# Third hop of a four-layer graph network: bias added on GpSimd, end rows formed in one VectorE operation, norm in place, and the output constant moved into VectorE's copy

## The chip, the cores and the metric

The kernel is one launch on one core of a Trainium2 chip. Times are microseconds (us) of that core. TensorE (PE; PEld is its weight load) multiplies and transposes and writes PSUM. VectorE (DVE), ScalarE (ACT) and GpSimd (POOL) do elementwise work; GpSimd also issues the indirect DMAs that gather and scatter rows, and SyncE (SP) issues the plain ones. "Slower" and "faster" speak of the time of the whole launch.

## The reference

Four layers work on 50,000 nodes of 128 features and 12,500 edges sorted by destination. Each is `x = x + layer(relu(layernorm(x)))`. Cut to what matters here:

```
x1 = x  + GCN3(h)          # 3 convolutions, then @ Wl + bl
m  = h[src] + edge_feats   # second layer: mean over the edges of a node,
h  = (1+eps)*h + mean(m)   # then two products with batch norms
x3 = x2 + 6 steps of  x += relu(mean(x[src]) @ Wh.T + bh)
out = x3 + (tanh(gcn_conv(h, W1, b1)) @ W2 + b2)
```

Only nodes that are the destination of an edge ("end rows") get anything but a dense product from a convolution. So the kernel treats all nodes as dense rows and computes the rows at edge ends again, by "hops" over the sorted edges.

## The kernel before, in words

Rows come in groups of 512 (four tiles of 128); "pairs" are two groups. Edges are 98 tiles of 128, in 14 iterations (`IT`) of 7 tiles, split 4 and 3 over two buffers b (`SUB`).

A first phase (to about 1200 us) runs a list of slots. Each has one dense pair (`turn`, `prod`, `rows`, `x1_rows`) and, in later slots, iterations of hops. The hops numbered 0, 1, 2 and 3 in the code are the first to fourth hop. Hop 0 has one iteration in a slot; hops 1 to 3 have two, and two slots without a hop stand ahead of each (`GAP`). The third hop (2) runs in seven slots between 820 and 1007 us, the fourth (3, "mean") in seven from 1037 us.

An iteration of a hop is: GpSimd gathers 7 tiles of neighbour rows (`h_G` and `h_M` by turns); VectorE makes messages of them (line 291) and, after TensorE's transposes, a running sum along the edges (line 315); TensorE multiplies back into `h_P` (line 326); VectorE scales by `dinvw` and adds a bias (`dve_affine`, line 335).

In the third hop the sum then gets the raw feature rows of the end node, `XD`, loaded by SyncE (`xd_load`), in a second VectorE operation (`x1_ends`, line 1279), and lands in `RS`, the resident array [128, 98, 128]. That is x1 at the edge ends. SyncE stores it; `m_moments` and `m_rstd` take its norm's statistics; ScalarE normalizes it into a buffer `HR` (`m_apply`), SyncE stores this (`m_store`), and ScalarE scales it by `vscale` back into `RS` (`m_scaled`, line 1004). The fourth hop's messages are gathered rows plus edge features (`FE`, line 295) plus that `RS` (line 298).

A second phase (to about 1800 us) runs the batch norms and is not touched. The last phase has the six steps and the last convolution: slots of one dense pair and two hop iterations again, a slot without a hop ahead of each step. The dense pair's rows are held in PSUM banks `XB`: TensorE adds the terms up there. In the slot after its own, a pair is turned (line 1936), multiplied (line 1943), gets the constant b2 from a small product of three rows `ones3` with `split_out` (`rows_const`, line 1947) and the product with `w32` (`rows`, line 1955). VectorE copies the bank to `O` (`rows_out`, line 2190), which SyncE stores. Each engine's program is written out in the order of the slot list; nothing is reordered later.

## Time and profile before

| | |
|---|---|
| time, median of 3 runs | 3171.38 us (3167.26 to 3177.81) |
| the profiled execution's own time | 3173.83 us |
| its span | 3172.1 us |
| PE busy | 2513.3 us, 79% of the span |
| DVE busy | 2030.2 us, 64% |
| ACT busy | 1971.6 us, 62% |
| POOL busy | 1440.7 us, 45% |

Busy shares over the whole span hide that the stages differ; each stage's engines are to be read by themselves, with what each waited for. "Idle before" in a row is how long the engine had stood still and whose work it then had waited for.

### The profile page before, as it was taken

To read this page: it belongs to the slowest core of one execution; us is meant where nothing else is said; L and a number is where in the kernel's file an instruction comes from. 1 tells how busy PE (TensorE), PEld (TensorE's weight loads), DVE (VectorE), ACT (ScalarE), POOL (GpSimd) and SP (SyncE) were. 2 spreads that over 40 slices of the span, in tenths; PEclk is the share of its full clock that TensorE was granted. 3 is DMA by queue.
4 is the path that set the end of the run, shared out by engine and by line. 5 is a ranking of instruction groups with operands and counts; after the bars stand their busy time and mean duration, and the time that the engine had idled before them with its cause. 6 is when DMAs were issued, how large, how long until landed. Compare 5 with 4: busy or idle time off the path is not lost. (4 is left out here: it accounts for less than half of the span.)

```text
span 3172.1 us, 46018 instructions
## 1 busy us (share of the span) xinstructions
PE 2513.3 (79%) x11251; PEld 1548.1 (49%) x11251; DVE 2030.2 (64%) x7784; ACT 1971.6 (62%) x4381; POOL 1440.7 (45%) x1507
## 2 busy tenths in 40 slices
PE   5787677787767788999999647899999999766840
PEld 2454444555555564444544323456565656444520
DVE  6655677788897662333333467787787878876620
ACT  1687777876777654555555478777767677755300
POOL 6666666365542640000000000567676766654576
PEclk8899888899877998999999758999999999977865
DMA  5666555455665653443334488665565656433311
GB/s 100 182 197 184 170 153 150 145 169 158 193 192 163 196 172 106 139 136 136 132 138 135 141 258 300 206 184 181 179 192 184 191 179 187 134 101 115 93 55 41
DMA packets 528965, 504.91 MB, mean 159 GB/s; under 512 B 58706, under 2 KB 389955, under 8 KB 528616
## 3 DMA queue, kind: packets, MB, share of 16 engines
q1 hardware_dynamic: 477388, 415.73, 40.8%
q0 software_dynamic: 47184, 85.73, 10.6%
q10 hardware_dynamic: 4172, 0.99, 0.2%
q8 instruction: 79, 1.29, 0.2%
q14 instruction: 142, 1.16, 0.1%
HBM read 246.45 MB, written 260.27 MB: 160 GB/s over the span
## 5 line engine op out<-in xcount | busy, mean ns | idle before, releaser
L1850 POOL DMA_INDIRECT h_G<-step_tab,row_i x294 | 286.8, 976 | 352.5 <-DMA step_tab<-l_NR 192.9
L800 PE MATMUL a_PA<-a_H,w 128*128 128x512 f32 x504 | 274.3, 674 | 89.4 <-ACT a_H L964 86.0
L1850 POOL DMA_INDIRECT h_M<-step_tab,row_i x294 | 285.2, 970 | 120.9 <-issue 86.6
L1563 DVE TENSOR_SCALAR b_Y<-b_BP,col 128x512 f32<-128x512 f32 x148 | 109.9, 742 | 354.4 <-PE b_BP L1517 354.4
L1545 ACT ACTIVATE b_Z<-b_BQ,bn 128x512 f32<-128x512 f32 x148 | 115.0, 777 | 257.3 <-PE b_BQ L1509 257.0
L1605 POOL TENSOR_TENSOR b_d<-b_d,neghalf 128x1 f32<-128x1 f32 x1 | 0.6, 565 | 592.2 <-DVE b_d L1596 592.2
L1517 PE MATMUL b_BP<-b_Z,w 128*128 128x512 f32 x592 | 266.3, 592 | 0.0
L270 POOL DMA_INDIRECT h_G<-msg_tab,row_i x147 | 143.0, 973 | 207.4 <-issue 111.4
L2217 DVE TENSOR_TENSOR_SCAN h_T<-keep,h_T,h_P 128x512 f32<-128x512 bf16 x196 | 222.9, 1137 | 12.2 <-PE h_P L1968 3.1
L239 ACT ACTIVATE a_HI<-a_X,a_ln_nm,a_ln_rs 128x128 f32<-128x128 f32 x490 | 201.0, 484 | 24.4 <-DVE a_ln_nm L222 24.4
L973 ACT ACTIVATE a_H<-a_PA,col 128x512 f32<-128x512 f32 x252 | 162.2, 668 | 82.7 <-PE a_PA L800 82.4
L800 PEld LDWEIGHTS a_PA<-a_H,w 128*128 128x128 f32 x504 | 96.2, 215 | 194.2 <-ACT a_H L964 115.7
L1989 PE MATMUL h_P<-wht,h_T 128*128 128x128 f32 x1176 | 185.4, 300 | 0.0
L270 POOL DMA_INDIRECT h_M<-msg_tab,row_i x147 | 139.5, 949 | 90.1 <-PE h_P L306 48.7
L208 ACT ACTIVATE l_ln_sd<-l_ln_mv,lneps 128x8 f32<-128x8 f32 (+1 forms) x136 | 41.0, 301 | 221.8 <-DVE l_ln_mv L2182 193.7
L1989 PEld LDWEIGHTS h_P<-wht,h_T 128*128 128x128 f32 x1176 | 152.2, 200 | 37.1 <-issue 35.0
L2224 DVE TENSOR_TENSOR h_Z<-h_P,inv_cnt 128x512 f32<-128x512 f32 (+1 forms) x168 | 103.4, 616 | 98.5 <-PE h_P L1989 98.5
L239 ACT ACTIVATE a_NR<-a_XR,a_ln_nm,a_ln_rs 128x128 f32<-128x128 f32 x392 | 155.9, 484 | 13.9 <-DVE a_ln_nm L222 13.5
L822 PE MATMUL a_P<-w3l,a_H 128*128 128x128 f32 x980 | 164.1, 317 | 0.0
L1517 PEld LDWEIGHTS b_BP<-b_Z,w 128*128 128x128 f32 x592 | 106.8, 190 | 106.6 <-issue 106.6
L2076 ACT ACTIVATE l_NR<-l_XB,l_ln_nm,l_ln_rs 128x128 f32<-128x128 f32 x392 | 141.8, 467 | 27.1 <-DVE l_ln_nm L2200 27.1
L822 PEld LDWEIGHTS a_P<-w3l,a_H 128*128 128x128 f32 x980 | 137.6, 217 | 31.5 <-issue 31.5
(385 smaller groups left out, 6452.3 us busy)
## 6 DMA issues: line engine op xcount, KB each, us to landing
b_HI<-hin_tab SPq DMA_DIRECT2D x148, 256.0 KB, 2.8
y_tab<-b_Y SPq DMA_DIRECT2D x148, 256.0 KB, 2.0
l_Y<-y_tab SPq DMA_DIRECT2D x148, 256.0 KB, 3.5
l_X<-x_tab SPq DMA_DIRECT2D x148, 256.0 KB, 4.5
x_tab<-a_X SPq DMA_DIRECT2D x112, 256.0 KB
hin_tab<-a_HI SPq DMA_DIRECT2D x112, 256.0 KB, 3.6
a_XR<-in_x SPq DMA_DIRECT2D x97, 256.0 KB, 4.3
out_rows<-l_O SPq DMA_DIRECT2D x97, 256.0 KB, 3.1
```

Source lines behind the costliest of these rows:

```text
L239: last = nc.scalar.activation(normed[:, k, :], rows[:, k, :], AF.Relu, scale=self.rs[:, c:c + 1], bias=self.nm[:, c:c + 1])
L270: pool.indirect_dma_start(out=GR_[i % 2][b][:, j, :], out_offset=None, in_=self.table[:, :], in_offset=bass.IndirectOffsetOnAxis(ap=row_i[ ...
L800: nc.tensor.matmul(PA[b][:, 0:nt * P], w[:, :], h[b][:, 0:nt, :].rearrange("p t d -> p (t d)"), start=True, stop=True).then_inc(done, 1)
L822: last = nc.tensor.matmul(P3[b][:, k * P:(k + 1) * P], H2[b][:, k, :], w3l[:, :], start=False, stop=(k == nt - 1))
L973: nc.scalar.activation(dst_h[b][:, 0:nt, :], PA[b][:, 0:nt * P], AF.Relu, bias=col[:, c:c + 1]).then_inc(done, 1)
L1517: last = nc.tensor.matmul(BP[b][:, :], w12[:, c, :], ZT[c][b][:, :], start=(c == 0), stop=(c == 1))
L1545: nc.scalar.activation(ZT[c][b][:, :], (BQ, BQ2)[c][b][:, :], AF.Relu, bias=bn1[:, 2 + c:3 + c], scale=bn1[:, c:c + 1]).then_inc(b_z[c], 1)
L1563: nc.vector.tensor_scalar(Y[b][:, :], BP[b][:, :], col[:, C_B12:C_B12 + 1], None, ALU.add).then_inc(b_y, 1)
L1850: pool.indirect_dma_start(out=GR_[i % 2][b][:, k, :], out_offset=None, in_=table[:, :], in_offset=bass.IndirectOffsetOnAxis(ap=row_i[:, t ...
L1989: last = nc.tensor.matmul(PH[b][:, k * P:(k + 1) * P], T[b][:, k * P:(k + 1) * P], wht[:, :], start=False, stop=(k == nt - 1))
L2076: last = nc.scalar.activation(to[:, k, :], rows, AF.Relu, scale=ln2.rs[:, c:c + 1], bias=ln2.nm[:, c:c + 1])
L2217: nc.vector.tensor_tensor_scan(T[b][:, 0:nt * P], keep[:, t * P:(t + nt) * P], PH[b][:, 0:nt * P], T[1 - b][:, w - 1:w], ALU.mult, ALU.add ...
```

## The change

Four edits:

1. GpSimd adds the bias `rb3l` to the loaded end rows `XD` in place, one operation for each half of an iteration (`biased`), behind the gathers of the same iteration in its queue.
2. `x1_ends` scales the product straight from PSUM and adds the biased `XD` in one operation per tile, written to `RS`; the operations of `dve_affine` into `h_Z` and of line 1279 are gone in the third hop. It waits for `xd_set` of GpSimd, and waits for its own end ahead of raising `h_out`.
3. `m_apply` normalizes `RS` in place, behind the store of x1; `m_scaled` is gone. The scaling by `vscale` moves into the fourth hop's messages on VectorE, one operation per tile, ahead of the addition of the edge features.
4. In the last phase `rows_const` is gone, and VectorE's copy of the bank becomes an addition of a resident constant `rb32` (b2 on all partitions, one more load at the start).

```diff
+    rb32 = sb(top, "rb32", [P, D])
...
-        def pool_gathers(self, pool):
+        def pool_gathers(self, pool, behind=None):
             for i in range(IT):
                 for b in range(2):
                     self.pool_gather(pool, i, b)
+                if behind:
+                    behind(i)
...
             if self.kind == "mean":
+                dve.wait_ge(mn.normed, 2 * i + b + 1)
+                for j in range(nt):
+                    last = nc.vector.scalar_tensor_tensor(rows[:, j, :], RS[:, t + j, :], vscale[:, t + j:t + j + 1], rows[:, j, :],
+                                                          ALU.mult, ALU.add)
+                last.then_inc(h_mid, 1)
+                dve.wait_ge(h_mid, 2 * i + b + 1)
                 dve.wait_ge(features_in[b], 16 * (i + 1))
-                nc.vector.tensor_tensor(rows[:, 0:nt, :], rows[:, 0:nt, :], features[b][:, 0:nt, :], ALU.add).then_inc(h_mid, 1)
-                dve.wait_ge(h_mid, 2 * i + b + 1)
-                dve.wait_ge(m_v, 2 * i + b + 1)
-                last = nc.vector.tensor_tensor(rows[:, 0:nt, :], rows[:, 0:nt, :], RS[:, t:t + nt, :], ALU.add)
+                last = nc.vector.tensor_tensor(rows[:, 0:nt, :], rows[:, 0:nt, :], features[b][:, 0:nt, :], ALU.add)
...
+            def biased(i):
+                for b, nt in enumerate(SUB):
+                    pool.wait_ge(xd_ld[2 * (i % 2) + b], 16 * (i // 2 + 1))
+                    rows = XD[i % 2][b][:, 0:nt, :]
+                    nc.gpsimd.tensor_tensor(rows, rows, rb3l[:, :].unsqueeze(1).broadcast_to([P, nt, D]), ALU.add).then_inc(xd_set, 1)
...
-                hop.pool_gathers(pool)
+                hop.pool_gathers(pool, biased if hop.h == 2 else None)
...
             def m_apply(i):
                 for b in range(2):
                     t = first_tile(i, b)
-                    after(act, m_v, 2 * (i - 1) + b + 1)
-                    after(act, m_h_st[b], 16 * i)
-                    mn.act_apply(act, i, b, _Rows(RS, t), HR[b])
-
-            def m_scaled(i):
-                for b, nt in enumerate(SUB):
-                    t = first_tile(i, b)
                     act.wait_ge(m_x1_st[2 * (i % 2) + b], 16 * (i // 2 + 1))
-                    act.wait_ge(mn.normed, 2 * i + b + 1)
-                    for k in range(nt):
-                        last = nc.scalar.activation(RS[:, t + k, :], HR[b][:, k, :], AF.Copy, scale=vscale[:, t + k:t + k + 1])
-                    last.then_inc(m_v, 1)
+                    mn.act_apply(act, i, b, _Rows(RS, t), _Rows(RS, t))
...
                 if k == GAP[3]:
-                    m_scaled(IT - 2)
                     m_apply(IT - 1)
-                    m_scaled(IT - 1)
...
                     n, use, t, nt = hop.at(i, b)
+                    dve.wait_ge(h_prod, n + 1)
+                    dve.wait_ge(xd_set, 2 * i + b + 1)
+                    for j in range(nt):
+                        last = nc.vector.scalar_tensor_tensor(RS[:, t + j, :], PH[b][:, j * P:(j + 1) * P], dinvw[:, t + j:t + j + 1],
+                                                              XD[i % 2][b][:, j, :], ALU.mult, ALU.add)
+                    last.then_inc(h_z, 1)
                     dve.wait_ge(h_z, n + 1)
-                    dve.wait_ge(xd_ld[2 * (i % 2) + b], 16 * (i // 2 + 1))
-                    nc.vector.tensor_tensor(RS[:, t:t + nt, :], Z[b][:, 0:nt, :], XD[i % 2][b][:, 0:nt, :], ALU.add).then_inc(h_out, 1)
+                    dve.sem_inc(h_out, 1)
...
-            def rows_const(j):
-                for b in range(2):
-                    nc.tensor.matmul(XB[j % 2][b][:, :], ones3[:, :], split_out[:, :], start=False, stop=False, skip_group_check=True)
...
-                nc.vector.tensor_copy(O[b][:, :, :].rearrange("p t d -> p (t d)"), XB[r][b][:, :]).then_inc(o_set, 1)
+                nc.vector.tensor_tensor(O[b][:, :, :], XB[r][b][:, :].rearrange("p (t d) -> p t d", d=D),
+                                        rb32[:, :].unsqueeze(1).broadcast_to([P, 4, D]), ALU.add).then_inc(o_set, 1)
```

VectorE's program in the first iteration of a third-hop slot, before: the tail of the hop iteration, then the messages of the next (`h_M`).

```order
L335 SCALAR_TENSOR_TENSOR h_Z<-h_P,dinvw,rb3l 128x128 [waits h_out,h_prod]
L335 SCALAR_TENSOR_TENSOR h_Z<-h_P,dinvw,rb3l 128x128 x3
L335 SCALAR_TENSOR_TENSOR h_Z<-h_P,dinvw,rb3l 128x128 [waits h_out,h_prod]
L335 SCALAR_TENSOR_TENSOR h_Z<-h_P,dinvw,rb3l 128x128 x2
L1279 TENSOR_TENSOR RS<-h_Z,a_XD 128x512 [waits xd_ld0,h_z]
L1279 TENSOR_TENSOR RS<-h_Z,a_XD 128x384 [waits xd_ld1,h_z]
L291 SCALAR_TENSOR_TENSOR h_M<-h_M,wE,RS 128x128 [waits h_got1_0]
```

VectorE at the same place now.

```order
L1279 SCALAR_TENSOR_TENSOR RS<-h_P,dinvw,a_XD 128x128 [waits xd_set,h_prod]
L1279 SCALAR_TENSOR_TENSOR RS<-h_P,dinvw,a_XD 128x128 x3
L1279 SCALAR_TENSOR_TENSOR RS<-h_P,dinvw,a_XD 128x128 [waits h_z,xd_set,h_prod]
L1279 SCALAR_TENSOR_TENSOR RS<-h_P,dinvw,a_XD 128x128 x2
L294 SCALAR_TENSOR_TENSOR h_M<-h_M,wE,RS 128x128 [waits h_z,h_got1_0]
```

The two additions over 512 and 384 columns are gone, and the second half and the next messages now stand behind a wait on VectorE's own last result (`h_z`).

GpSimd's queue where the third hop begins, before: gathers only.

```order
L270 DMA h_G<-msg_tab,row_i 128x128 [waits r2_st1,h_st1,h_turn,r2_st0,h_st0]
L270 DMA h_G<-msg_tab,row_i 128x128 x3
L270 DMA h_G<-msg_tab,row_i 128x128 [waits h_turn]
L270 DMA h_G<-msg_tab,row_i 128x128 x2
L270 DMA h_M<-msg_tab,row_i 128x128 [waits h_turn]
L270 DMA h_M<-msg_tab,row_i 128x128 x3
```

GpSimd's queue at the same place now.

```order
L271 DMA h_G<-msg_tab,row_i 128x128 [waits r2_st1,h_st1,h_turn,r2_st0,h_st0]
L271 DMA h_G<-msg_tab,row_i 128x128 x3
L271 DMA h_G<-msg_tab,row_i 128x128 [waits h_turn]
L271 DMA h_G<-msg_tab,row_i 128x128 x2
L743 TENSOR_TENSOR a_XD<-a_XD,rb3l 128x512 [waits xd_ld0]
L743 TENSOR_TENSOR a_XD<-a_XD,rb3l 128x384 [waits xd_ld1]
L271 DMA h_M<-msg_tab,row_i 128x128 [waits h_turn]
```

Two additions, each waiting for a load of `XD`, now stand between the gathers of one iteration and those of the next.

TensorE's program in a slot of the last phase, before: the late pair's turn and product, its constant, and the hop iteration's products.

```order
L1936 MATMUL l_PC<-ident,l_NR 128x128 x8
L1943 MATMUL l_PC<-l_HT,w 128x512 x2
L1947 MATMUL l_XB<-split_out,ones 128x512 x2
L1979 MATMUL h_P<-l_VB,l_LH 128x512
L1989 MATMUL h_P<-wht,h_T 128x128 x4
L1979 MATMUL h_P<-l_VB,l_LH 128x384
```

TensorE at the same place now.

```order
L1940 MATMUL l_PC<-ident,l_NR 128x128 x8
L1947 MATMUL l_PC<-l_HT,w 128x512 x2
L1979 MATMUL h_P<-l_VB,l_LH 128x512
L1989 MATMUL h_P<-wht,h_T 128x128 x4
L1979 MATMUL h_P<-l_VB,l_LH 128x384
```

Only the two products of the constant are gone; the hop's first product (which waits for VectorE's running sum) now stands right behind the late pair's product.

## Rows read from the trace of the kernel before

**Rows 1.** Busy us (instructions) of PE, PEld, DVE, ACT, POOL; PE clock, DMA, GB/s.

```profile
820.00:1007.00 187.00, 132.56 (x642) 103.83 (x641) 171.94 (x739) 134.60 (x355) 80.99 (x86) 0.78 0.61 181
1007.00:1037.00 30.00, 22.11 (x101) 14.24 (x101) 15.72 (x96) 27.16 (x71) 9.45 (x10) 0.89 0.57 164
1037.00:1195.00 158.00, 122.05 (x722) 92.13 (x722) 107.46 (x342) 96.36 (x263) 85.45 (x88) 0.92 0.61 180
2000.00:2720.00 720.00, 684.50 (x3620) 427.97 (x3619) 577.61 (x2021) 518.82 (x1084) 496.22 (x510) 0.99 0.59 182
```

**Rows 2.** Timeline of VectorE in one third-hop slot: start, us, idle before.

```profile
907.79 1.90 DVE L335 SCALAR_TENSOR_TENSOR h_Z<-h_P,dinvw,rb3l 128x128 f32<-128x128 f32 x7
...
909.61 1.15 DVE L1279 TENSOR_TENSOR RS<-h_Z,a_XD 128x512 f32<-128x512 f32 x2
...
910.67 1.92 DVE L291 SCALAR_TENSOR_TENSOR h_M<-h_M,wE,RS 128x128 f32<-128x128 f32 x7
...
922.86 0.87 DVE L335 SCALAR_TENSOR_TENSOR h_Z<-h_P,dinvw,rb3l 128x128 f32<-128x128 f32 x3 [0.15 <-PE h_P L326]
```

**Rows 3.** Timeline of GpSimd's queue in the same slot: first and last gathers.

```profile
900.34 0.94 POOL L270 DMA_INDIRECT h_G<-msg_tab,row_i  x1 [5.47 <-PE h_P L306]
...
907.83 0.94 POOL L270 DMA_INDIRECT h_G<-msg_tab,row_i  x1 [0.30 <-issue]
...
912.79 0.94 POOL L270 DMA_INDIRECT h_M<-msg_tab,row_i  x1 [4.02 <-PE h_P L306]
...
927.38 0.94 POOL L270 DMA_INDIRECT h_G<-msg_tab,row_i  x1 [6.15 <-PE h_P L306]
```

**Rows 4.** SyncE's timeline: the load of end rows; then its line L575's landing time.

```profile
915.80 1.10 SPq L575 DMA_DIRECT2D a_XD<-xd_tab  x2
...
DMA to landing us min/median/max: 3.5/4.5/6.4
```

**Rows 5.** Lines L697 and L1605: the nearest GpSimd work, ns min/median/max.

```profile
L697 POOL MEMSET h_T<- x2: 514/516/519, 5.1 to 5.6; 128x512 f32 x2
...
L1605 POOL TENSOR_TENSOR b_d<-b_d,neghalf x1: 565/565/565, 1799.1 to 1799.1; 128x1 f32<-128x1 f32 x1
```

**Rows 6.** Timeline of ScalarE, then TensorE, behind the third hop's last step.

```profile
1017.01 2.15 ACT L1004 ACTIVATE RS<-a_SN,vscale 128x128 f32<-128x128 f32 x7
1019.06 2.80 ACT L239 ACTIVATE a_SN<-RS,m_ln_nm,m_ln_rs 128x128 f32<-128x128 f32 x7
1021.75 2.15 ACT L1004 ACTIVATE RS<-a_SN,vscale 128x128 f32<-128x128 f32 x7
...
1024.43 5.32 PE L800 MATMUL a_PA<-a_H,w 128*128 128x512 f32 x8 [5.46 <-ACT a_H L964]
```

**Rows 7.** VectorE's longest wait of the fourth hop, and its timeline there.

```profile
DVE h_G L295 <- DMA a_R<-in_edge_attr: 27.8, 6, 6.8
...
1082.14 0.69 DVE L295 TENSOR_TENSOR h_G<-h_G,a_R 128x512 f32<-128x512 f32 x1 [3.44 <-DMA a_R<-in_edge_attr]
1082.87 0.69 DVE L298 TENSOR_TENSOR h_G<-h_G,RS 128x512 f32<-128x512 f32 x1
```

**Rows 8.** Timeline of VectorE and TensorE in two slots of the last phase.

```profile
2121.56 2.35 DVE L2217 TENSOR_TENSOR_SCAN h_T<-keep,h_T,h_P 128x512 f32<-128x512 bf16 x2
...
2123.51 0.60 PE L1947 MATMUL l_XB<-split_out,ones 3*128 3x512 bf16 x2
2123.95 0.38 PE L1979 MATMUL h_P<-l_VB,l_LH 24*128 24x512 bf16 x1
...
2311.40 0.60 PE L1947 MATMUL l_XB<-split_out,ones 3*128 3x512 bf16 x2
...
2311.94 0.39 PE L1979 MATMUL h_P<-l_VB,l_LH 48*128 48x512 bf16 x1
```

**Rows 9.** Timeline of TensorE in a slot without a hop.

```profile
2140.36 0.60 PE L1947 MATMUL l_XB<-split_out,ones 3*128 3x512 bf16 x2
2141.49 2.05 PE L1955 MATMUL l_XB<-w,l_HT 128*128 128x128 f32 x16 [0.53 <-ACT l_HT L2091]
```

More of the change, by code:

```diff
@@ L455, in build @@
     sp_f, sp_r = (XDW[1][0:1, b, :, :] for b in range(2))
-    HR, MH, FE = SN[0], R1, R2
+    MH, FE = R1, R2
     PA, P3 = [ps(ctx, f"a_PA{b}") for b in range(2)], [ps(ctx, f"a_P3{b}") for b in range(2)]
@@ L489, in build @@
                                                   sems("r2_st", 2))
-    xd_got, xd_st, xd_ld, wd_set, m_x1_st, m_h_st, m_v = ([sems(f"xd_got{k}", 2) for k in range(2)], [sems(f"xd_st{k}", 2) for k in range(2)], sems("xd_ld", 4),
-                                                                 sem("wd_set"), sems("m_x1_st", 4), sems("m_h_st", 2),
-                                                                 sem("m_v"))
+    xd_got, xd_st, xd_ld, wd_set, m_x1_st, m_h_st = ([sems(f"xd_got{k}", 2) for k in range(2)], [sems(f"xd_st{k}", 2) for k in range(2)], sems("xd_ld", 4),
+                                                            sem("wd_set"), sems("m_x1_st", 4), sems("m_h_st", 2))
+    xd_set = sem("xd_set")
     feat_in, feat_pad, mh_st, mh_ones = sems("feat_in", 2), sem("feat_pad"), sems("mh_st", 2), sem("mh_ones")
@@ L496, in build @@
     REST = E - FULL * P
-    N_LOADS = 29
+    N_LOADS = 30
     padded = [(t, base) for t in (hin_tab, x1_tab) for base in (E0, S0)]
@@ L593, in m_store @@
                     sp.wait_ge(mn.normed, 2 * i + b + 1)
-                    sp.dma_start(edge_rows(msg_tab[3], RR, first_tile(i, b), nt), HR[b][:, 0:nt, :]).then_inc(m_h_st[b], 16)
+                    t = first_tile(i, b)
+                    sp.dma_start(edge_rows(msg_tab[3], RR, t, nt), RS[:, t:t + nt, :]).then_inc(m_h_st[b], 16)
             def raw_store(i):
@@ L915, in _ @@
                      (rbl[:, :], b0l.partition_broadcast(P)), (rbh[:, :], bh.partition_broadcast(P)),
+                     (rb32[:, :], b32.partition_broadcast(P)),
                      (w01[:, :], W01[:, :]), (w02[:, :], W02[:, :]),
@@ L1059, in _ @@
                         sn.act_std(act, i + 1)
-                    if hop.h == 2 and i > 1:
-                        m_scaled(i - 2)
                     if hop.h == 2 and u:
@@ L1343, in _ @@
                         m_rstd(i - 1)
-                    if hop.h < 3:
+                    if hop.h < 2:
                         for b in range(2):
@@ L1361, in _ @@
                         m_rstd(i - 1)
-                    if hop.h < 3:
+                    if hop.h < 2:
                         for b in range(2):
@@ L1954, in rows @@
                     for k in range(4):
-                        last = nc.tensor.matmul(XB[j % 2][b][:, k * P:(k + 1) * P], HT[b][:, k, :], w32[:, :], start=False, stop=(k == 3), skip_group_check=True)
+                        last = nc.tensor.matmul(XB[j % 2][b][:, k * P:(k + 1) * P], HT[b][:, k, :], w32[:, :], start=False, stop=True, skip_group_check=True)
                     last.then_inc(p2_set, 1)
@@ L2018, in _ @@
                     prod(late)
-                if late is not None:
-                    rows_const(late)
                 for i in its[:1]:
```

## The prediction

> **What bounds the kernel now.** I read the span in stretches first, since 79% for TensorE is a mean over stages with different limits. In the third hop (820 to 1007 us) VectorE is busy 171.94 of 187 us, 92%, with TensorE at 132.56, ScalarE at 134.60 and GpSimd at 80.99 [rows 1]. In the steps of the last phase (2000 to 2720 us) TensorE is busy 684.50 of 720 us, 95%, at a granted clock of 0.99, and VectorE 577.61, 80% [rows 1]. Between them lie two stretches in which no engine is near that, and there the waits decide: in the slots without a hop (1007 to 1037 us) ScalarE is busy 27.16 of 30 us [rows 1], and in the fourth hop (1037 to 1195 us) VectorE waits 27.8 us for the loads of edge features, in 6 waits of up to 6.8 us [rows 7].
>
> Then I read one slot of the third hop in the timeline. A slot repeats after 27.04 us (gathers of the same kind at 900.34 and 927.38) [rows 3], and VectorE runs through it almost without a gap: seven operations of line 335, the pair of line 1279, then the next messages [rows 2]. So what leaves VectorE there shortens the slot, as long as nothing else comes to stand ahead of it.
>
> **The change part by part.** The sum is made against the profiled execution's 3173.83 us (span 3172.1 and 1.7 around it).
>
> *Third hop, VectorE.* Line 335 keeps its seven operations in an iteration (1.90 us for seven) with another operand and another target [rows 2]; the price of one stays, since it read PSUM and one array of SBUF before and does so now. The pair of line 1279 goes: from 909.61 to 910.67, 1.06 us [rows 2]. Added are two waits on VectorE's own last result in each iteration. Without such a wait an operation begins 0.08 us before the one ahead of it is shown to end (907.79 + 1.90 against 909.61) [rows 2]; with it, 0.04 us after (1082.14 + 0.69 against 1082.87) [rows 7]. So each costs 0.12 us. An even iteration saves 1.06 - 0.24 = 0.82 us. In an odd one the second half waits 0.15 us for TensorE anyway [rows 2], which hides one of the waits: 0.94 us. Seven slots: 7 x 1.76 = 12.3 us. Raising `h_out` this way costs no more than the wait counted.
>
> *Third hop, GpSimd.* It gets 28 additions, 512 and 384 columns wide. The trace of before has none of this size. The nearest rows are a memset of 128x512 in 0.516 us, one stream of the array, and a tensor operation on a single column in 0.565 us, which is nearly all fixed cost [rows 5]. From below the wide addition takes 0.52 us; from above three streams and the fixed cost, 3 x 0.516 + 0.565 = 2.1 us. I take 1.3 us, the middle, and 1.0 us for 384 columns, since the two reads may or may not overlap. With 0.30 us between instructions [rows 3] an iteration's pair is 2.9 us.
> The Trainium skill, "GPSIMD Engine Reference", section 3.1, gives 4497 ns for such an addition of 2048 columns; scaled to 512 and 384 that is an estimate of 1.1 and 0.8 us, so about 2.5 us for the pair with the gaps. No run here shows it yet.
>
> Is there room? A gather takes 0.94 + 0.30 us, seven 8.7 us, so GpSimd works 17.4 of the 27.04 us and stands still for 5.47 and 4.02 us [rows 3]. With both pairs it works 23.2 us, in a slot that shrinks to 25.3. But the additions wait for loads. The load for iteration i+2 is issued at 915.80, 5.1 us after the sum of iteration i (910.67) [rows 2, 4], and lands 4.5 us later (up to 6.4) [rows 4], so at about 921; the gathers of i+2 are done at 908.8, and those of i+3, which could have begun at 912.79 [rows 3], now stand behind the additions. They run from 923 to 932 and land by 936 even at 3.5 us (as for the loads of rows 4). Their messages are due one slot after 910.67, at 937.7 before, at 936 now. GpSimd thus loses most of its lead, but it is not late; and the load itself comes earlier, since it stands behind `m_store` in SyncE's queue, which waits for ScalarE's norm, and that starts up to 2.05 us earlier without `m_scaled` ahead of it. I count nothing. If that cover were gone, the next messages would be late, and with them the scan behind them.
> `m_apply` in place waits for the store of x1 to land. That store is issued right after the sum and is done well before the norm's statistics come back, so it costs nothing.
>
> *Between the third and the fourth hop, ScalarE.* At 1017.01, 1019.06 and 1021.75 it scales, normalizes and scales; TensorE then stands still for 5.46 us, until 1024.43, for the line 964 copy behind them [rows 6]. Each scaling occupies 2.05 us (1017.01 to 1019.06). Both go, and TensorE's wait shrinks by 4.1 us, leaving 1.4. The 14 other scalings (of 28 halves, 2.05 us for each iteration) lie beside VectorE's 92% and are worth nothing directly.
>
> *Fourth hop, VectorE.* In place of two additions for each half (0.69 us for 512 columns) [rows 7] stand one addition and one operation per tile, at 1.90/7 = 0.27 us each [rows 2]. That is about +0.6 us for an iteration, 14 x 0.6 = 8.5 us in all. But the order changed too: the tile operations now come before the wait for the features, and the waits of up to 6.8 us, 3.44 in the slot shown [rows 7], take them in; behind the wait only one addition is left in place of two, so the first half's messages are ready 0.7 us sooner. The second half and the second iteration are later by up to 1.2 us a slot, in front of a wait again. I take zero, with -3 and +8.5 us as ends.
>
> *Last phase, TensorE.* The two products of the constant take 2123.51 to 2123.95, 0.44 us, and 0.54 us in a later step (2311.40 to 2311.94) [rows 8]; the 0.10 more may belong to what follows, so I take 0.44. What stands behind them waits for the first half of VectorE's scans; both scans began at 2121.56 and took 2.35 us, so the first half was done near 2122.7, before 2123.51 [rows 8]. So the wait does not take up the gain. 35 slots of the first five steps have a late pair and two iterations: 35 x 0.44 = 15.4 us, at most 35 x 0.54 = 18.9. In the slot without a hop TensorE waits 0.53 us for ScalarE's tanh behind the constant [rows 9], so those give nothing, and in the last step and the last hop, where TensorE is no longer the full engine, I count nothing either. VectorE's copy from PSUM becomes an addition from PSUM with one array of SBUF, 98 times; line 1279 and line 298 show such additions at 0.6 to 0.7 us [rows 2, 7], the price of the copy. The extra load at the start is one of thirty small ones: nothing.
>
> Sum: 3173.8 - 12.3 - 4.1 - 15.4 = 3142.0 us. The profiled execution was 2.4 us above the median of the runs; against it 1.4 us for collisions of GpSimd with VectorE (below). I forecast **3141 us**, 30 us less.
>
> **The rivals.**
> *GpSimd becomes the bound of the third hop (slower; 10%).* One slot of GpSimd is 17.4 us plus two pairs of additions. It passes the 25.3 us of VectorE when a pair takes more than 3.9 us with its gaps, 1.65 us for one addition; the upper bound (2.1 us, and 1.7 for 384 columns) gives slots of 26.2 us, and 6 of the 12 us lost. The whole 31 us are gone when the slot is 25.3 + 31/7 = 29.7 us, at 2.8 us for one addition, and at 3.1 us the kernel is 10 us slower than before, 3182. For it speaks that the trace shows no such operation and that loads and additions now stand in one line; against it both rows of GpSimd's price. Half of this case ends within or above 0.3% of before.
>
> *GpSimd's additions and VectorE hold each other up (6%).* The only VectorE operations here with two arrays in SBUF are the messages, 14 x 0.27 = 3.8 us of a slot. If each of 28 additions met one and held it for its own 1.15 us, that would be 32 us and the time 3173, no change. By shares of time 3.8 of 25 us meet, some 4 additions, 5 us at most. The Trainium skill, "SBUF — State Buffer", section "SBUF: two separate sides", states such a rule: the pair of ports that VectorE and GpSimd share is an exclusive lock, taken by a VectorE operation with two SBUF inputs against a GpSimd operation that reads SBUF. The trace of before has no pair of such operations to test it.
>
> *The last phase gives half or less (13%).* ScalarE's chain (tanh, relu of the next rows, norm) may end last once TensorE is 0.44 us sooner; it already ends last in the slots without a hop [rows 9]. Then 8 us of the 15 stay away: 3149.
>
> *The fourth hop keeps its extra VectorE work (8%).* If the waits for features move along with the messages, +8.5: 3150.
>
> *More than counted (5%):* the 0.54 us and a shorter fourth hop: below 3134.
>
> **How the numbers follow.** The case as summed has 58%, with a range of its own from 3134 to 3149. The range 3132 to 3159 takes in the rivals of the last phase and the fourth hop, and the milder half of GpSimd's; about 15% are left out. A measurement of this kernel tells 0.3%, 9.5 us, from no change: faster means below 3162. Slower holds only the dear end of GpSimd's case: 5%; same holds the rest of it and the worst of the collisions: 7%; faster 88%.
>
> **What would show each step right or wrong.** Third hop: slots of 25.3 us, VectorE still above 90% busy, and no wait of VectorE for gathers or for GpSimd's additions; the additions' own duration is the first number to read, 1.3 us or not. Between the hops: TensorE's wait of 5.46 us down to about 1.4. Fourth hop: its 158 us unchanged, tile operations ahead of the wait for features. Last phase: slots 0.44 us shorter in each of 35, TensorE still near 95%. Wrong would be: GpSimd full in the third hop, or TensorE's share falling there by as much as its work.

## The result, and the profile after

The changed kernel took 3159.24 us (median of 20 runs, 3150.30 to 3176.71) against 3177.14 of the kernel before on the same chips: a ratio of 0.9957 with a 95% interval of 0.9943 to 0.9971, so 14 us less (9 to 18) where 30 were forecast; the two medians themselves differ by 17.9. Two later comparisons on other chips gave 0.9943 (0.9918 to 0.9968) and 0.9927 (0.9906 to 0.9948), 18 and 23 us. All three intervals lie below 1, so it is faster, by half to three quarters of the forecast. The profiled execution had 3156.34 us and a span of 3154.6.

The four stretches of [rows 1], now (by windows; columns as there):

```profile
833.90:1007.50 173.60, 123.37 (x614) 95.55 (x614) 152.89 (x684) 102.74 (x256) 106.34 (x109) 0.81 0.66 194
1007.50:1037.50 30.00, 21.85 (x108) 13.07 (x108) 18.70 (x107) 27.24 (x66) 9.56 (x11) 0.99 0.65 195
1037.50:1190.00 152.50, 118.68 (x713) 89.21 (x714) 113.92 (x401) 92.28 (x254) 85.89 (x88) 0.93 0.60 180
2000.00:2715.00 715.00, 665.51 (x3530) 424.97 (x3529) 580.01 (x2008) 516.16 (x1076) 494.43 (x508) 0.99 0.59 183
```

In the third hop VectorE fell from 92% busy to 88% (152.89 of 173.60 us): it lost work, and also began to wait. In the steps TensorE fell from 95% to 93% (665.51 of 715): its removed products left idle time behind. The prediction wanted VectorE above 90% and TensorE near 95%; TensorE's share falling by as much as its work is what it had said would show it wrong.

VectorE and then GpSimd in a third-hop slot (timeline), to be held against [rows 2, 3]:

```profile
912.58 1.12 DVE L1279 SCALAR_TENSOR_TENSOR RS<-h_P,dinvw,a_XD 128x128 f32<-128x128 f32 x4 [0.16 <-PE h_P L332]
913.92 0.87 DVE L1279 SCALAR_TENSOR_TENSOR RS<-h_P,dinvw,a_XD 128x128 f32<-128x128 f32 x3 [0.21 <-PE h_P L332]
914.93 1.93 DVE L294 SCALAR_TENSOR_TENSOR h_M<-h_M,wE,RS 128x128 f32<-128x128 f32 x7
...
908.96 2.21 POOL L743 TENSOR_TENSOR a_XD<-a_XD,rb3l 128x512 f32<-128x512 f32 x2 [1.39 <-DMA a_XD<-xd_tab]
...
922.78 2.22 POOL L743 TENSOR_TENSOR a_XD<-a_XD,rb3l 128x512 f32<-128x512 f32 x2 [2.88 <-DMA a_XD<-xd_tab]
```

From the first end row to the next messages VectorE takes 914.93 - 912.58 = 2.35 us; it was 910.67 - 907.79 = 2.88 [rows 2]. So 0.53 us went in this iteration, not 0.82: between 913.70 (912.58 + 1.12) and 913.92 it stands still for 0.21 us, and ahead of the messages for 0.14 (from 913.92 + 0.87 to 914.93), where the order has its waits on its own last result. The first of the two stands is put down to TensorE in the row, but it is 0.21 us in each of 13 iterations, whatever is named. Over these iterations the stretch lasted 3.08 us in the mean before, with waits for TensorE in it, and lasts 2.35 in every one now: 0.73 less. Each addition pair of GpSimd takes 2.2 us and waits for its load, and no row of VectorE waits for it.

How long each stage was is read from SyncE's stores. Two rows of the changed kernel by line (first and last start stand before the semicolon): the stores of x1 at the edge ends, and of the steps' rows.

```profile
L620 SPq DMA_DIRECT2D x_tab<-RS x28: 359/370/377, 833.9 to 1007.5; - x28
L1797 SPq DMA_DIRECT2D step_tab<-RS x140: 370/378/1739, 2016.7 to 2685.4; - x140
```

The same reading of these profiles gives this table (us; worked out from such rows). Third hop: first to last x1 store (13 intervals of its 14 iterations). Gap: from there to the first store of the fourth hop. Fourth: to the start of the second phase. Steps: first to last of the 140 step stores (five steps). Last hop: to the last store of its table. End: to the last output store.

| kernel | third hop | gap | fourth | steps | last hop | end |
|---|---|---|---|---|---|---|
| before | 178.9 | 42.4 | 152.3 | 671.6 | 192.2 | 104.7 |
| only_12 | 175.1 | 43.6 | 153.2 | 665.9 | 187.8 | 102.3 |
| only_3 | 178.9 | 40.8 | 146.5 | 669.6 | 186.8 | 102.8 |
| only_123 | 174.1 | 40.7 | 149.6 | 667.7 | 188.0 | 102.0 |
| only_4 | 177.6 | 43.1 | 149.2 | 672.4 | 188.8 | 98.9 |
| features_behind | 178.5 | 43.2 | 147.8 | 667.3 | 191.0 | 105.2 |
| fewer_gathers | 179.4 | 42.4 | 154.7 | 658.5 | 192.7 | 102.1 |
| fewer_gathers_edit4 | 177.5 | 43.1 | 152.5 | 641.0 | 188.7 | 101.5 |
| changed, three profiles | 173.6, 172.3, 173.1 | 41.2, 42.3, 40.5 | 148.6, 149.1, 150.1 | 668.7, 671.3, 672.4 | 186.5, 186.7, 186.1 | 98.6, 99.4, 98.5 |

A stage that an edit doesn't touch scatters by 1 to 6 us in it. The start of the third hop, behind code that all kernels share, lies anywhere from 825 to 847 us, so the total of a single execution tells little, and a stage far more.

### The profile page after: what moved, and what is told of

It reads as the page before. It is cut to its first block and busy times, and to the rows that moved or that the text cites. A ratio compares the mean times of both kernels' runs of the same rounds, so it can differ in the third digit from the quotient of the medians.

```text
span 3154.6 us, 45769 instructions
## 1 busy us (share of the span) xinstructions
PE 2483.1 (79%) x11153; PEld 1536.1 (49%) x11153; DVE 2034.3 (64%) x7826; ACT 1943.0 (62%) x4283; POOL 1472.6 (47%) x1535
## 5 line engine op out<-in xcount | busy, mean ns | idle before, releaser
L271 POOL DMA_INDIRECT h_M<-msg_tab,row_i x147 | 140.9, 959 | 64.9 <-issue 40.8
```

Of the source, the lines that this page charges most:

```text
L271: pool.indirect_dma_start(out=GR_[i % 2][b][:, j, :], out_offset=None, in_=self.table[:, :], in_offset=bass.IndirectOffsetOnAxis(ap=row_i[ ...
```

## The experiments

### Each edit alone

> The change without its last edit: third and fourth hop as changed, the constant again from TensorE and the plain copy. If the steps of the last phase end with GpSimd's gathers (98 of 1.25 us in each), edit 4 gave nearly nothing there and this kernel holds most of the gain: 9 to 14 us under before. If the gain of the change came mainly from the last phase (as predicted, 15 us there), this kernel is within 5 us of before.

> Before with the last edit alone. GpSimd theory: the five steps take the same 138 us each, and 0 to 6 us are gained in all, in the last step and the last hop, where other engines than GpSimd end last. The prediction's own step: 15 us, 35 slots shorter by 0.44 us.

> Before with GpSimd's additions and the one-operation ends of the third hop alone. Seven slots of the third hop shorter by 1.3 us each where a wait of VectorE on its own tile operations costs 0.29 us (0.21 of standing and the lost overlap of 0.08): 7 to 9 us under before. If GpSimd's additions hold the slots up by themselves (they wait for loads), the stage is no shorter than 3 us, and VectorE waits for gathers or for the biased rows.

> Before with the norm in place and the scaling moved to VectorE's messages alone. Between the hops 4 us less (two scalings off ScalarE), the fourth hop unchanged or 3 us shorter: 4 to 7 us under before. If the fourth hop pays for its 98 added operations less 28 additions, it is 5 to 8 us longer and the kernel is not faster.

Each takes the named edits of the diff onto the kernel before. Measured, as ratios to the kernel before, all on one chip: only_123 0.9957 (0.9939 to 0.9974), only_4 1.0001 (0.9982 to 1.0020), only_12 0.9972 (0.9951 to 0.9993), only_3 0.9969 (0.9950 to 0.9988). In us about -14, 0, -9 and -10. So the edit that carried half of the forecast gives nothing that these runs can tell (its interval reaches from -6 to +6 us), and the first three give what there is.

### Why the output constant gave nothing: fewer gathers

In the kernel before, GpSimd's queue in one step of the last phase begins and ends so (timeline; the first rows and the last, and the next step's first):

```profile
2140.00 0.95 POOL L1850 DMA_INDIRECT h_G<-step_tab,row_i  x1 [15.39 <-issue]
2141.26 0.95 POOL L1850 DMA_INDIRECT h_G<-step_tab,row_i  x1 [0.30 <-issue]
...
2264.22 0.95 POOL L1850 DMA_INDIRECT h_M<-step_tab,row_i  x1 [0.30 <-issue]
2278.40 0.95 POOL L1850 DMA_INDIRECT h_G<-step_tab,row_i  x1 [13.23 <-issue]
```

98 gathers follow each other with 0.30 us between them and wait for nothing, 125.2 us from 2140.00 to 2265.17; then GpSimd stands still for 13.23 us, until the step's last rows are stored, and the next step begins. That is 17.9 us for the 14 gathers of a slot, where an undisturbed slot of TensorE (from one late pair's product to the next) took 17.37 us. TensorE looked full because it was only just behind. In the changed kernel its undisturbed slots take 16.84 us, 0.53 less, and GpSimd's gathers follow each other as before, so this can't come through. The experiment relieves GpSimd (the waits for the gathers count 3 to match); a seventh of the gathered rows is left out:

```diff
-                    for k in range(nt):
+                    for k in range(nt if i >= F0 else 3):
```

> The kernel before, with 6 gathers in place of 7 for each iteration of the six steps (a seventh of the neighbour rows is left out, the rest of the work stays). GpSimd's gathers then take 7 x 12 x 1.253 = 105 us of a step in place of 122.8. Theory (in the steps GpSimd's queue and TensorE are nearly equal bounds, 17.55 and 17.37 us a slot): TensorE is bound alone, and 7 x 0.18 = 1.3 us come off a step, 0 to 8 us in the six. Rival (GpSimd has slack, TensorE alone is the bound, as the prediction had it): no change. This run sets the base for the next one.

> The same kernel with fewer gathers, and edit 4 (the output constant in VectorE's copy, TensorE's products of the constant gone). Theory (GpSimd's gathers took up edit 4's gain): with GpSimd relieved the slots shorten by the 0.54 us that single slots of the changed kernel showed, 35 x 0.54 = 19 us below fewer_gathers, 15 to 19 and a few more from the slots of the last step. Rival (ScalarE's chain of tanh, relu and norm ends last once TensorE is sooner, the prediction's rival for this phase): under 8 us, as edit 4 alone gave 1.6 us.

Measured: 0.9977 (0.9956 to 0.9997) and 0.9900 (0.9874 to 0.9926). Edit 4 on top of fewer gathers takes the time to 0.9923 of what it was (0.9900 / 0.9977), 24 us less (some 14 to 35 by the two intervals), where alone it took none. The five steps went from 658.5 to 641.0 us, 17.5 us or 0.50 for each of 35 slots, as the trace of TensorE had promised. Fewer gathers also mean less work for the DMA engines; but a gather still starts 1.26 us after the one ahead of it (median of each step, as before), so it is the number of gathers on the queue that changed. In fewer_gathers_edit4 GpSimd waits for TensorE (its waits from 1990 to 2690 us: total, times, longest):

```profile
POOL h_G L1852 <- DMA step_tab<-RS: 104.5, 5, 22.1
...
POOL h_G L1852 <- PE h_P L1966: 21.1, 19, 1.4
POOL h_M L1852 <- PE h_P L1966: 10.1, 23, 0.5
```

With all its gathers it is TensorE that waits; in the changed kernel, 1990 to 2715 us (in the kernel before these two rows are 9.3 and 0.2 us, and with fewer gathers there are none):

```profile
PE h_P L1968 <- DMA h_G<-step_tab,row_i: 15.4, 12, 2.2
...
PE h_P L1968 <- DMA h_M<-step_tab,row_i: 5.1, 13, 0.8
```

### The third hop: GpSimd's part

> The changed kernel without the 28 additions on GpSimd (the bias of the third layer is left out of the end rows; their one operation on VectorE waits for the load itself). It prices what edit 1 costs in total: GpSimd's time, its waits for loads, and any holding up of VectorE. Theory (GpSimd has room in the third hop, 23 of 26 us of a slot): no change against the changed kernel, within 3 us. Rival (GpSimd is the bound there or holds VectorE up): the missing part of the third hop's forecast comes back, 6 us or more below the changed kernel.

> The changed kernel with each GpSimd addition made twice, the second behind the end of the first (the bias is added twice). A pair of additions then takes 2 x 1.26 + 2 x 0.99 us and the gaps, near 5.7 us in place of 2.9, and GpSimd's slot 17.4 + 11.4 = 28.8 us against 26.3 us now. Theory (the forecast's rival, seen from its deciding point of 3.9 us a pair): GpSimd becomes the bound, slots of 28.8 us or more (the waits for loads come on top), 7 x 2.5 = 17 us above the changed kernel, 15 to 35. Rival (loads and gathers are far enough ahead to take it in): under 5 us.

```diff
 no_pool_addition
-                    nc.gpsimd.tensor_tensor(rows, rows, rb3l[:, :]..., ALU.add).then_inc(xd_set, 1)
-                    dve.wait_ge(xd_set, 2 * i + b + 1)
+                    dve.wait_ge(xd_ld[2 * (i % 2) + b], 16 * (i // 2 + 1))
 pool_addition_twice
-                    nc.gpsimd.tensor_tensor(rows, rows, rb3l[:, :]..., ALU.add).then_inc(xd_set, 1)
+                    for half in range(2):
+                        nc.gpsimd.tensor_tensor(rows, rows, rb3l[:, :]..., ALU.add).then_inc(xd_mid if half == 0 else xd_set, 1)
+                        if half == 0:
+                            pool.wait_ge(xd_mid, 2 * i + b + 1)
```

Without the additions (the bias is left out): 0.9957 (0.9938 to 0.9977), third hop 174.1 us, the same as the changed kernel. Twice: 0.9981 (0.9961 to 1.0001), third hop 182.6 us, some 9.5 us more. But not for the reason expected. Two pairs in a row take 4.64 us, GpSimd works about 26.7 of a slot of 28.1 us, and VectorE waits for an addition only 0.6 us in all. What grew is VectorE's busy time for the same 684 instructions, from 152.9 to 153.9 us in the three profiles of the changed kernel to 166.1. Its timeline and GpSimd's there:

```profile
928.80 0.88 DVE L223 SCALAR_TENSOR_TENSOR a_ln_nm<-a_ln_mv,a_ln_rs 128x8 f32<-128x8 f32 x1
929.60 0.19 DVE L216 RECIPROCAL m_ln_r<-m_ln_sd 128x7 f32<-128x7 f32 x1
929.83 0.93 DVE L218 TENSOR_TENSOR m_ln_rs<-m_ln_r,isend 128x7 f32<-128x7 f32 x1
...
926.09 4.64 POOL L744 TENSOR_TENSOR a_XD<-a_XD,rb3l 128x512 f32<-128x512 f32 x4
```

Operations of 7 and 8 columns that take 0.17 us elsewhere last 0.88 and 0.93, the second until 930.76, where GpSimd's additions end at 930.73. The reciprocal between them, with one operand, is not held.

### The third hop: VectorE's own waits

> The changed kernel, with VectorE's waits on its own last results in the third hop taken off its path: the end rows raise h_out themselves, and the wait for them stands behind the next messages' first half (or, where none follow, in the slot behind). In the trace of the changed kernel each of the 28 waits costs 0.21 us of standing still and 0.08 us of lost overlap. Theory: 28 x 0.29 = 8 us, less the 7 that wait for TensorE anyway, so 6 to 8 us below the changed kernel, about 3153. Rival (the third hop is by now held by TensorE's and ScalarE's products as well as by VectorE): half or less comes through, 0 to 3 us. Wrong for both if it is slower than the changed kernel.

```diff
-                    last.then_inc(h_z, 1)
-                    dve.wait_ge(h_z, n + 1)
-                    dve.sem_inc(h_out, 1)
+                    last.then_inc(h_out, 1)
```

(The wait for `h_out` and the raising of `h_z` stand behind the first half of the next messages.) Measured 0.9963 (0.9943 to 0.9983), third hop 172.5 us: nothing came through. VectorE's waits in that stretch, first of the kernel before, then of this one:

```profile
DVE h_Z L335 <- PE h_P L326: 6.4, 22, 0.6
DVE a_ln_mv L202 <- DVE a_ln_st L193: 2.6, 13, 0.5
DVE m_ln_mv L202 <- DVE m_ln_st L193: 2.1, 12, 0.2
DVE a_X L1237 <- PE a_P L822: 0.7, 1, 0.7
```

```profile
DVE a_ln_r L216 <- ACT a_ln_sd L209: 5.1, 6, 1.2
DVE a_X L1236 <- PE a_P L834: 4.6, 5, 1.8
DVE RS L1279 <- PE h_P L332: 3.5, 15, 0.6
```

The waits that appear are for the dense pair of the same slot: its standard deviation on ScalarE and its last product on TensorE. Both stand behind the end rows' norm in ScalarE's program, which the next experiment moves.

### The third hop: ScalarE's order, and where the additions fall

> The kernel with deferred waits, and one move on ScalarE: where a third-hop slot ends, the norm of the last end rows (7 tiles, 2.8 us) goes behind TensorE's copies and the standard deviation of the next dense pair in place of ahead of them. With the deferred waits VectorE stood 5.1 us in 6 waits for that deviation, and 4.6 us in 5 for TensorE's dense products behind ScalarE. Theory (the third hop's missing gain waits behind ScalarE's order): the 13 intervals of the third hop go from 172.5 to 166 to 169 us, 3 to 6 us below the changed kernel in time. Rival (VectorE, TensorE and ScalarE are in step by now, so that a wait removed comes back as another): 171 us or more, no change.

> late_norm with the two GpSimd additions of an iteration put behind the gathers of the next iteration, 8.7 us later. In the trace of late_norm an addition ran from 900.16 to 902.38 us, and two norm operations of VectorE (7 and 8 columns) took 1.07 and 0.81 us there in place of 0.17; 14 such cases came to 9.3 us in the hop. From 906.2 to 914 us VectorE does statistics and scans there, which have one operand in SBUF or take the other from PSUM. Theory (they hold each other up): the small operations are back at 0.17 us and the 13 intervals of the third hop go from 172.0 to 163 to 166 us. Rival 1 (the additions now come too late for the end rows, due at 915.25): VectorE waits for GpSimd, 172 us or more. Rival 2 (the engines are in step): the small operations are short, but waits take their place, 170 to 172 us.

> late_norm without GpSimd's additions (the third layer's bias is left out of the end rows). It removes every meeting of GpSimd's additions with VectorE. Theory (they hold each other up): 163 us for the 13 intervals of the third hop, and no VectorE operation of 7 or 8 columns above 0.3 us. Rival (the engines are in step): 170 to 172 us with longer waits of VectorE for ScalarE or TensorE.

> late_norm with GpSimd's addition of half an iteration made tile by tile (4 and 3 operations of 128 columns in place of one of 512 and one of 384). From 1.27 us for 512 and 0.99 for 384 columns one of 128 is near 0.45 us, the seven 3.2 us. In late_norm a small VectorE operation with two operands in SBUF lasted until the GpSimd addition beside it ended, up to 1.22 us. Theory (it can begin between two of GpSimd's operations): none of them lasts over 0.6 us, the 9.3 us of holding up fall to about 4, and the 13 intervals of the third hop to 168 to 170 us, 2 to 4 us below late_norm. Rival (GpSimd's next operation takes over without a gap, or the longer run of additions meets more of them): as much or more held up, 172 us or more.

```diff
 late_norm
                 if s:
                     ln2.act_std(act, s - 1)
+                if waiting:
+                    m_apply(waiting.pop())
...
-                        m_apply(i - 1)
+                        waiting.append(i - 1) if u else m_apply(i - 1)
 late_add
-                if behind:
-                    behind(i)
+                if behind and i:
+                    behind(i - 1)
+            if behind:
+                behind(IT - 1)
 tile_adds
-                    nc.gpsimd.tensor_tensor(rows, rows, rb3l[:, :]..., ALU.add).then_inc(xd_set, 1)
+                    for j in range(nt):
+                        last = nc.gpsimd.tensor_tensor(rows[:, j, :], rows[:, j, :], rb3l[:, :], ALU.add)
+                    last.then_inc(xd_set, 1)
```

late_norm holds the deferred waits of own_wait_deferred too. The other three are late_norm with one thing more: the additions put later, left out (and the bias with them), or made tile by tile. Each was compared with the kernel before on its own chip.

| kernel | ratio to before | third hop | VectorE busy | held up |
|---|---|---|---|---|
| own_wait_deferred | 0.9963 (0.9943 to 0.9983) | 172.5 | 151.8 | 0.6 |
| late_norm | 0.9955 (0.9932 to 0.9979) | 172.0 | 159.5 | 9.3 |
| late_add | 0.9965 (0.9945 to 0.9985) | 178.1 | 168.9 | 13.3 |
| late_no_add | 0.9952 (0.9931 to 0.9974) | 167.6 | 150.5 | 0.0 |
| tile_adds | 0.9934 (0.9913 to 0.9954) | 167.0 | 157.5 | 8.0 |

"Held up" is what the norm's small operations took above 0.167 us each. For late_norm it comes from these rows of VectorE's groups (count, busy, mean ns): 13 x 0.342 + 12 x 0.282 + 13 x 0.115 = 9.3 us.

```profile
L218 DVE TENSOR_TENSOR m_ln_rs<-m_ln_r,isend 128x7 f32<-128x7 f32 x13 | 6.6, 509 | 0.4
L223 DVE SCALAR_TENSOR_TENSOR a_ln_nm<-a_ln_mv,a_ln_rs 128x8 f32<-128x8 f32 x12 | 5.4, 449 | 0.4
L223 DVE SCALAR_TENSOR_TENSOR m_ln_nm<-m_ln_mv,m_ln_rs 128x7 f32<-128x7 f32 x13 | 3.7, 282 | 0.4
```

The move on ScalarE did take VectorE's waits away: for the deviation 5.1 to 1.8 us, for the dense product 4.6 to 1.1. What came in their place is GpSimd. The timeline of one slot of late_norm, VectorE and then GpSimd:

```profile
900.38 1.07 DVE L223 SCALAR_TENSOR_TENSOR a_ln_nm<-a_ln_mv,a_ln_rs 128x8 f32<-128x8 f32 x1
901.38 0.19 DVE L216 RECIPROCAL m_ln_r<-m_ln_sd 128x7 f32<-128x7 f32 x1
901.60 0.81 DVE L218 TENSOR_TENSOR m_ln_rs<-m_ln_r,isend 128x7 f32<-128x7 f32 x1
902.45 0.17 DVE L223 SCALAR_TENSOR_TENSOR m_ln_nm<-m_ln_mv,m_ln_rs 128x7 f32<-128x7 f32 x1
...
900.16 2.22 POOL L743 TENSOR_TENSOR a_XD<-a_XD,rb3l 128x512 f32<-128x512 f32 x2 [3.04 <-DMA a_XD<-xd_tab]
```

The pair of additions runs to 902.38; the first small operation ends near the seam of the two (901.45), the second at 902.41, and the third, begun behind it, takes its 0.17 us. The Trainium skill, "SBUF — State Buffer", section "SBUF: two separate sides", says that a VectorE operation with two SBUF inputs and a GpSimd operation that reads SBUF exclude each other, and that the later one waits for the whole of the earlier. By that rule the trace agrees here. In late_norm all 14 lengthened operations end 0.02 to 0.03 us behind an addition.

Putting the additions 8.7 us later (late_add) was meant to take them out of the way. It went the other way: in five of 13 iterations they met the last small operation of the norm, and it lasted 2.76 to 2.88 us, until both additions were over (timeline, VectorE and then GpSimd):

```profile
898.94 2.76 DVE L223 SCALAR_TENSOR_TENSOR m_ln_nm<-m_ln_mv,m_ln_rs 128x7 f32<-128x7 f32 x1
901.62 1.89 DVE L1284 SCALAR_TENSOR_TENSOR RS<-h_P,dinvw,a_XD 128x128 f32<-128x128 f32 x7
...
899.44 2.22 POOL L745 TENSOR_TENSOR a_XD<-a_XD,rb3l 128x512 f32<-128x512 f32 x2
```

The small operation shows its start 0.50 us ahead of the first addition here, 0.5 to 0.6 in all five cases, and is held nevertheless. By the starts that the profile shows, "the later one waits" doesn't cover this; why it is held from there stays open. In six more iterations the additions fell on the messages, which also have two arrays in SBUF: one operation of 0.35 us lasted 0.81 to 2.79, 5.7 us in all, on top of the 13.3 of the table.

None of the three outcomes written down beforehand was this one: the additions were not late for the end rows, they fell on another place. Without additions (late_no_add) the hop takes 167.6 us, 4.4 less than late_norm: of 9.3 us held up, 5 came back as waits for TensorE's products. So both answers to the open question were half right. tile_adds reached 167.0 us, but not as expected: the small operations were held for 8.0 us, one of them for 1.58, and what fell is VectorE's idle time (167.0 - 157.5 = 9.5 us, against 12.5 in late_norm and 17.1 in late_no_add). Why it fell is not shown.

### Side by side

> The changed kernel, beside the next two on one chip: 14 to 18 us below before, the third hop's 13 intervals at 172.3 to 173.6 us as in its two profiles so far.

> late_norm again: third hop at 172 us and 9 us of holding up, no faster than the changed kernel, if its first profile stands; if another profile differs by more than 2 us, the meetings of the two engines come by chance.

> tile_adds again. If shorter additions are what helps: 167 us again for the third hop, and 4 to 6 us below the changed kernel. If the first profile was chance: 170 to 173 us, and no difference from the changed kernel.

On one chip: the changed kernel 3155.89 us, 0.9927 (0.9906 to 0.9948); late_norm 3163.71, 0.9960 (0.9942 to 0.9978); tile_adds 3149.79, 0.9908 (0.9886 to 0.9929). Third hop 173.1, 170.5 and 169.6 us; held up 1.2, 9.2 and 8.3. So the meetings repeat and aren't chance. Of the 5.0 us by which the hop of tile_adds was shorter than that of late_norm, 0.9 came again, with VectorE idle 11.7 us against 11.5: the gain over late_norm is not settled. The hop of tile_adds is 3 to 6 us shorter than that of the changed kernel in both profiles. In time it lay 6 us below the changed kernel here, but the intervals overlap: it surely beats the kernel before, and whether it beats the changed one is not settled. late_norm was slower here than its stages explain (its third hop is shorter, the other stages alike); that stays open.

### The fourth hop's order

> The kernel before with the two additions of the fourth hop's messages exchanged: the one of the scaled end rows first, then the wait for the edge features and their addition. Nothing is removed. Theory for the gain of edit 3 beyond the 4 us between the hops (VectorE waited 27.8 us for features there, and with edit 3 only one addition is left behind that wait): an addition of 0.69 us in each of the 14 iterations' first halves moves ahead of the wait, 4 to 7 us below the kernel before. Rival (ScalarE's missing scalings free the fourth hop's start, order is worth nothing): no change.

```diff
-                dve.wait_ge(features_in[b], 16 * (i + 1))
-                nc.vector.tensor_tensor(rows[:, 0:nt, :], rows[:, 0:nt, :], features[b][:, 0:nt, :], ALU.add).then_inc(h_mid, 1)
-                dve.wait_ge(h_mid, 2 * i + b + 1)
                 dve.wait_ge(m_v, 2 * i + b + 1)
-                last = nc.vector.tensor_tensor(rows[:, 0:nt, :], rows[:, 0:nt, :], RS[:, t:t + nt, :], ALU.add)
+                nc.vector.tensor_tensor(rows[:, 0:nt, :], rows[:, 0:nt, :], RS[:, t:t + nt, :], ALU.add).then_inc(h_mid, 1)
+                dve.wait_ge(h_mid, 2 * i + b + 1)
+                dve.wait_ge(features_in[b], 16 * (i + 1))
+                last = nc.vector.tensor_tensor(rows[:, 0:nt, :], rows[:, 0:nt, :], features[b][:, 0:nt, :], ALU.add)
```

Measured 0.9994 (0.9973 to 1.0015). The interval reaches from -9 to +5 us and so can't tell 4 us from none. The stage says a little more: 147.8 us, against 149.2 to 154.7 of the five kernels that keep the old order and 146.5 to 150.1 of those with edit 3 in the table. That fits the order alone shortening the fourth hop, but it is one profile, 1.4 us below the lowest of the old order, and the two groups overlap; so it is not shown.

## Why the prediction was half right

The predicted 3141 us is 18 us too low, and the median lies just above the range. 5.8 of these 18 us lie in the kernel before, which took 3177.14 us in this comparison and 3171.38 when the forecast was made; the rest is gain that did not come. By the stages the three profiles of the changed kernel differ from the mean of the kernels without the edit concerned by -5.9 us (third hop, for all 14 iterations), -1.7 (gap), -3.1 (fourth), +2.4 (steps), -2.7 (last hop) and -4.6 (end): -15.6 in all, which fits the measured 14 to 23.

*Last phase, -15.4 forecast: wrong, and this is the step that failed.* "TensorE is no longer the full engine" was said of the wrong part. In the 35 slots it counted, TensorE's undisturbed slot did shrink by 0.53 us, more than the 0.44 taken, but GpSimd's gathers were a bound just as near: the steps did not get shorter. In the 13 profiles with edit 4 and all gathers they take 668.7 to 675.8 us, 671.9 in the mean, against 665.9 to 671.6, 668.4 in the mean, in the five without it; why they are rather longer is not shown. Where nothing was counted, at the end, 4.6 us came (95.3 to 99.4 us with edit 4, 102.0 to 105.2 without). The two nearly cancel, as the run of edit 4 alone says. The 2.7 us of the last hop lie inside the 186.8 to 192.7 us of the kernels without edit 4 and can't be put down to it. Most of the number was on the table: 510 gathers in 720 us [rows 1], at the 0.94 + 0.30 us used for the third hop [rows 3], are 632 us. With the five stands of 13 to 15 us at the ends of steps, which the same trace shows, it is 700 of 720. Read as busy share alone, 496.22 of 720, GpSimd looks 69% full. The rival for this phase named ScalarE; fewer_gathers_edit4 shows that it was GpSimd.

*Third hop on VectorE, -12.3 forecast, -5.9 measured: the mechanism right, the size off.* The pair of line 1279 went and VectorE's busy time fell by 11 us. But its idle time rose from 15 to 19 or 21 us. Two things took the rest. Its own waits cost 0.29 us between the halves and 0.22 ahead of the messages (0.21 and 0.14 of standing still, and each time the lost overlap of 0.08), not 0.12 each; even so the stretch from the first end row to the next messages got 0.73 us shorter in the mean, 9.5 us in 13 iterations, since waits for TensorE inside it went as well. And some 4 of these 9.5 us came back as waits for the dense pair of the slot (its deviation from ScalarE and its product from TensorE: 3.9 to 5.7 us in the three profiles, 0 to 0.7 in the four kernels without edits 1 and 2 and with all gathers). Taking the own waits off the path gave nothing for the same reason. The whole forecast, 12.3 x 13/14 = 11.4 us, does come through once three things are out of the way: late_no_add has 178.5 - 167.6 = 10.9, with the own waits deferred, ScalarE's order changed and no additions.

*GpSimd's additions.* Duration right: 1.27 and 0.99 us (1.3 and 1.0 taken). That they fit and wait for loads: right. "GpSimd becomes the bound" did not happen, and at double the work the hop grew by 9.5 us through holding VectorE up. *Collisions, 1.4 us counted:* 0.3, 1.0 and 1.2 us in three profiles (0.1 in only_123, 3.1 in only_12), right in size, partly by luck; but the text named only the messages as VectorE operations with two arrays in SBUF, and those hit were the norm's operations of 7 and 8 columns, which it had overlooked. The messages were hit in late_add. The small share of time of the norm's operations is no measure of the risk: they follow each other at one place of a slot, and when the slot shifts they are hit in most iterations (9 of 13 in late_norm).

*Between the hops, -4.1:* TensorE's wait went from 5.46 us to 2.51 (1.4 expected), the gap by 1.7. The row of after:

```profile
1021.69 3.89 PE L812 MATMUL a_PA<-a_H,w 128*128 128x512 f32 x8 [2.51 <-ACT a_H L977]
```

*Fourth hop, 0 (-3 to +8.5):* -3.1, at the good end, in a stage that scatters by 5 us without the edit. VectorE's waits for features there fell from 27.8 us [rows 7] to 23.7, with VectorE busier (113.92 us against 107.46 in [rows 1]). *m_apply in place, the extra load, VectorE's copy as an addition:* nothing lost, as forecast. ScalarE waits for no store of x1 in the profile of the changed kernel, and the addition takes the 0.68 us of the copy.

## What to carry to other kernels

Judge an engine that issues DMAs by the start-to-start distance of its instructions times their number, not by its busy share: 69% busy was full here, and an engine at 95% beside it hid that. Before work is taken off the fullest engine, price the second one by the same slot. When GpSimd gets tensor work beside VectorE, list every VectorE operation with two SBUF operands, the tiny ones too, and look in the new timeline whether they fall on it.

## What the runs showed of the hardware

A VectorE operation of 7 columns that takes 0.17 us lasted up to 2.88 us beside GpSimd additions (late_add, at 968.00 us), and ended within 0.06 us of an addition's end; whether it can get in at the seam of two additions varies (it did at 901.45 us in late_norm, not at all in late_add). One-operand operations, statistics and scans were not lengthened there. Seven GpSimd additions of 128 columns take 2.9 us together, 0.45 us for the mean one, against 2.2 us for one of 512 and one of 384; five more operations thus cost 0.7 us, near 0.15 us for each (an estimate). A gather of 128 rows costs its queue 1.25 us from start to start even when nothing is waited for. A wait of VectorE on its own result just written costs 0.21 us of standing still between two halves of the end rows and 0.14 to 0.15 ahead of the messages, and each time the overlap of 0.08.
